# Filler products on TensorE in three waits of an audio-tower kernel (one core)

## The reference

```python
h = conv1d(x, W_embed, 7 taps, pad 3) + b_embed          # 64 x 32 x 4096
h = einsum('oc,bcl->bol', W_proj, fold16(h)) + b_proj     # 64 x 128 tokens x 256 channels
h = h + mamba(layernorm(h))      # W_in 256->1024, 4-tap conv, silu, selective scan over 128
                                 # tokens with 16 states, gate silu(z), W_out 512->256
n = layernorm(h)
gates = softmax(n @ w_gate); top 2 of 8 experts
h = h + sum over the chosen e of gate_e * (silu(n @ wg[e]) * (n @ wi[e])) @ wo[e]
```

## Time and profile before

| | us |
|---|---|
| median of 3 runs | 2648.08 (2647.75 to 2649.83) |
| the profiled execution | 2650.71 |
| its span, first to last instruction | 2648.9 |
| mean granted TensorE clock, as a share of full speed | 0.989 |

### The profile page before, as it was taken

The page is one execution under the profiler, slowest core; times in us unless marked ns, Lnnn a source line. Parts: engine busy times, 40 slices in busy tenths (PEclk is TensorE's granted clock), DMA queues, the critical chain, the costliest instruction groups (busy, mean ns, idle before and its releaser), DMA issues. The chain is left out here.

```text
span 2648.9 us, 35497 instructions
## 1 busy us (share of the span) xinstructions
PE 2469.8 (93%) x10678; PEld 1511.3 (57%) x10679; DVE 2025.5 (76%) x2052; ACT 1559.3 (59%) x3388; POOL 1929.2 (73%) x823
## 2 busy tenths in 40 slices
PE   4899999999999999999999999987599999999998
PEld 2334444444444444444444444433599999999998
DVE  1699999999999999999999999999333333333333
ACT  2677777777777777777777777764222222222222
POOL 2698999999999999999999999998322222222222
PEclk9999999999999999999999999999699999999999
DMA  2331414324143141431414314132532223222322
GB/s 44 141 116 43 157 39 154 116 59 158 38 154 117 58 158 38 154 120 55 158 38 154 122 53 156 39 141 88 189 47 48 46 46 48 46 47 46 47 47 33
DMA packets 124947, 235.85 MB, mean 89 GB/s; under 512 B 46031, under 2 KB 93170, under 8 KB 108460
## 3 DMA queue, kind: packets, MB, share of 16 engines
q1 hardware_dynamic: 96384, 199.06, 22.3%
q0 software_dynamic: 26272, 34.44, 7.7%
q10 hardware_dynamic: 2188, 1.15, 0.2%
HBM read 181.83 MB, written 53.65 MB: 89 GB/s over the span
## 5 line engine op out<-in xcount | busy, mean ns | idle before, releaser
L561 POOL TENSOR_TENSOR arena<-u,arena 128x2048 f32<-128x2048 f32 x255 | 1156.4, 4535 | 44.9 <-DVE psum L1180 41.2
L1180 DVE TENSOR_TENSOR_SCAN psum<-psum,arena 128x1024 f32<-128x1024 f32 x416 | 951.1, 2286 | 64.2 <-POOL arena L557 51.8
L1642 PE MATMUL psum<-hc,ident 128*128 128x512 f32 x1664 | 800.1, 605 | 95.0 <-DVE hc L1214 94.9
L891 ACT ACTIVATE psum<-delta,a_neg 128x508 f32<-128x508 f32 x1024 | 654.5, 670 | 0.0
L652 POOL DMA_INDIRECT out_dram<-hres,tok_id x135 | 210.6, 1560 | 548.1 <-ACT hres L1107 371.5
L1642 PEld LDWEIGHTS psum<-hc,ident 128*128 128x128 f32 x1664 | 298.1, 190 | 491.5 <-issue 290.7
L1214 DVE TENSOR_TENSOR hc<-psum,arena 128x1024 f32<-128x1024 f32 x416 | 507.8, 1221 | 9.9 <-PE psum L1642 0.9
L1481 DVE TENSOR_TENSOR z<-psum,xn 128x512 f32<-128x512 f32 x135 | 93.3, 691 | 432.6 <-issue 320.4
L1107 ACT ACTIVATE hres<-psum,tok_w 128x256 f32<-128x256 f32 x135 | 64.1, 475 | 400.4 <-PE psum L1817 382.6
L885 ACT ACTIVATE psum<-zeros 128x8 f32<-128x8 f32 x512 | 89.5, 175 | 303.4 <-DVE hc L1214 258.0
L1804 PE MATMUL psum<-xnt,yz 128*128 128x128 f32 x2160 | 264.9, 276 | 0.0
(11 more groups left out here) (219 smaller groups left out, 2840.5 us busy)
## 6 DMA issues: line engine op xcount, KB each, us to landing
arena<-ssm_rows SPq DMA_DIRECT2D x128, 1024.0 KB, 5.8
delta<-expert_rows SPq DMA_DIRECT2D x135, 129.0 KB, 2.0
h_saved_rows<-hnew SPq DMA_DIRECT2D x16, 512.0 KB, 6.8
hres<-h_saved_rows SPq DMA_DIRECT2D x16, 512.0 KB, 3.5
out_dram<-h SPq DMA_DIRECT2D x16, 512.0 KB, 2.9
arena<-in_L_ffn_wg_dram SPq DMA_DIRECT2D x8, 512.0 KB, 10.2
arena<-in_L_ffn_wi_dram SPq DMA_DIRECT2D x8, 512.0 KB, 10.8
arena<-in_L_ffn_wo_dram SPq DMA_DIRECT2D x8, 512.0 KB, 10.8
```

The costliest lines, as they stand in the source:

```text
L561: pool.tensor_tensor(dBx[k % 2], rep, b_rep[:, q * QN:(q + 1) * QN, :], ALU.mult).then_inc(dbx_ready, 1)
L891: last = nc.scalar.activation(o, d, ACT.Exp, scale=a_neg[:, c, n:n + 1])
L1180: nc.vector.tensor_tensor_scan(out_, h, src, 0.0, ALU.mult, ALU.add).then_inc(scan_done, 1)
L1642: last = nc.tensor.matmul(yacc[c % 2], ident[:, :], state[:, i, :], start=False, stop=(nth_sum[k] == LAST_SUM[c] and i == 1))
```

## The change

A helper issues `n` products of the identity with itself into bank 4 of `psum`, 128 columns. Nothing reads them and they signal nothing. It is called three times: 64 products ahead of TensorE's first work, behind a wait for all nine constants (it was one constant, and stood behind the wait for the transfers); 46 after the embedding of group 0 and ahead of `turn_xn(0, 0)`; and 42 behind the waits for `tab_ready` and `w_loaded`, ahead of `turn_tile(0, 0)`.

```diff
         def _(pe):
 
+            def keep_turning(n):
+
+                for _ in range(n):
+                    nc.tensor.matmul(psum[:, 4, 0:P], ident[:, :], ident[:, :], start=True, stop=True)
+
+            pe.wait_ge(s_const, 9)
+            keep_turning(64)
             pe.wait_ge(s_emb, 16 * N_EMB)
-            pe.wait_ge(s_const, 1)
             pe.wait_ge(s_band0, 3)
...
                 for m in range(2):
                     embed(0, m)
+                keep_turning(46)
                 pe.wait_ge(emb_free, 1)
                 for k in range(NK):
                     turn_xn(0, k)
...
             pe.wait_ge(tab_ready, 1)
             pe.wait_ge(w_loaded, 16 * 3 * E)
+            keep_turning(42)
```

## The result

| | before | after |
|---|---|---|
| median of 20 runs, us | 2649.57 (2646.9 to 2651.77) | 2652.91 (2651.0 to 2654.87) |
| ratio after / before | | 1.0013 (95%: 1.0007 to 1.0019) |
| span of the profiled execution, us | 2648.9 | 2652.8 |
| mean granted TensorE clock | 0.989 | 0.989 |

The change costs 0.13%, 3.3 us (95%: 1.9 to 5.0). The interval leaves out zero, but the cost is less than the 0.2% that the prediction took as no change. The spans of the two profiled executions differ by 3.9 us, and two places make all of it. Each trace is one execution: the one before took 2650.71 us, 1.1 above the median of its kernel, and the one after 2654.59, 1.7 above.

What follows compares the result with a forecast made beforehand. TensorE was taken as the bound from the first tile to the end, so delays show in full: front 1.9 plus first tile 0.3 makes 2.2 us later, 2650.3 from 2648.08; range 2645.5 to 2654, likeliest case 2648 to 2652.5.

Steps and rivals of the forecast that it cites:

- the overrun of the second call: Front: 46 fillers end at 45.4, turn_xn another 2.8 us late, but hidden because group 1's windows land only at 53.1.
- rival B: Front: clock falls again in TensorE's 2.9 us wait for group 1's landing; sum 4.9 us, 2653.0; chance 0.23.
- Price of a filler: All three calls: two records a product, 0.223 us at high clock, plus 0.477 us per low-clock microsecond, taken as 5.4.
- Rivals A: All three calls: clock does not rise on identity products or only on real work; about 37 us slower, 2685; chance 0.06.
- C: All three calls: a product leaves one record, so prices are half; sum -2.5 us, 2645.6; chance 0.09.
- The chain to SP's issues: Front: first call delays group 0's turning to end at 31.9 against 28.42, so SP's issues and landing are 3.4 us later.
- Behind the fillers the clock is high: Front after the first call: work runs at the high clock, with embeddings at 1.12 us each for 2.07 and 2.04.
- the overrun is hidden behind SP's transfers: Front: projection ends at 50.2, windows land at 53.1; without that cover the second call would cost 2.8 us.
- L1518 was to move with L349: Sign for group 1: L349 at about 31.9, L1518 at 53.1 behind a transfer; wrong if L1518 does not move with it.
- The stretch to the convolution: Front, from group 1's landing to the convolution: 2.65 us at the high clock instead of 4.12, a gain of 1.45.
- The first tile: Third call, ahead of tile 0: 3.2 us late, 2.9 gained by the high clock, net 0.3 us later.
- What lies between: From the front's end to tab_ready: unchanged time, no wait has slack to take up the front's delay.

Runs made afterwards that it cites:

- kernel with the waits filled: The changed kernel with 13 more products in five short waits between the first call and the second; 2653.12 us, ratio 1.0010.
- fitted kernel: Changed kernel with calls of 30, 32, 27 products, waits filled with 3, 13, 3, 3, 3, and 25 ahead of group 1's turning; 2645.83 us, ratio 0.9986.
- fitted kernel with separate memory: The fitted kernel with group 1's windows in memory of their own and 11 products instead of 25 ahead of their turning; 2647.18 us, ratio 0.9990.
- two queues: Fitted kernel with separate memory, half of group 1's issues on POOL, no products ahead of group 1's turning; 2649.85 us, ratio 1.0000.

## Why the prediction was right, and where it was not

- **Sign and size**: 2650.3 from a median of 2648.08 was +2.2 us; measured +3.3 (1.9 to 5.0), and 2652.91 is inside the range. Of the 2.6 us between 2650.3 and 2652.91, 1.5 lie in the median of the kernel before, which was 2648.08 over 3 runs and 2649.57 over 20. The sign came out right because the first and the third call last longer than the waits that they stand in, by prices that the traces bear out. What the prediction held to be hidden, the overrun of the second call, was not.
- **Luck in a number**: rival B gave 2653.0, almost the measured time, but by a fall of the clock in a wait for the landing that did not exist in the changed kernel. That match means nothing.
- **Price of a filler**: two records, 0.223 us at the high level and 0.477 us for each microsecond at the low one. First call 16.9 predicted, 17.2 and 17.0 measured; third 12.0, and 12.1 and 12.2 measured. Rivals A (37 us) and C (-2.5) are out by this. The first call's 128 records took 16.05 to 17.18 us over five traces, so 16.9 is good to about 1 us.
- **The chain to SP's issues**: 31.9 predicted, 32.03 and 31.89. That the landing follows at a fixed distance (21.3 us) held in the kernel with the waits filled: 31.33 to 52.76, 21.4.
- **The step that failed**: "Behind the fillers the clock is high", on which the embeddings at 1.12 each rest, and from it "the overrun is hidden behind SP's transfers". The clock fell at 32.4, 5.4 us after the call had ended, in a stretch in which TensorE worked in short groups between copies of ScalarE. The embeddings took 2.07 and 2.04, the second call 12.99 for 10.3, and the overrun came out 1.4 us beyond the landing. The front was 3.59 us late for 1.9 predicted, and this is most of the difference. One of the prediction's own signs of being wrong was met: L1518 was to move with L349, and moved 5.12 us (49.72 to 54.84) for 3.57. Filling the waits took the 1.4 us away in both traces, though not measurably in the time. Rival B had the fall, but at another place.
- **The stretch to the convolution**: 2.65 predicted, 2.59 measured.
- **The first tile**: 3.2 late, 2.9 back, 0.3 net predicted and read in the trace after; 0.4 net with the third call alone.
- **What lies between**: that no wait behind the front takes up its delay held: 1829.77 and 1829.75 us from the convolution to the last table instruction.
- The Trainium skill's rule that the full clock does not engage for transposes, "TensorE: Matmul & The Clock Gate", Part 4: the runs speak against it here. Four transposes take 0.60 us at 26.86 where they took 1.12 at 19.20.

## What to carry to other kernels

A filler must end before the work it precedes, at the low clock's price: compute its length as products at the high level plus the loss of the first 3 to 6 us at the low one (what the traces here show), and if in doubt take fewer. A filler call only helps if the clock is still up where the long products stand; where the work between is sparse, small fillers in the waits can hold it, as they did here in the traces. The fitted kernel has both, shorter runs and fillers in the waits, and which of the two gives how much of its 3.7 us was not measured apart. And look at what else waits behind the delayed engine: here TensorE began its first work 7.7 us late, and 3.6 us of that reached the end through a queue of transfers that nobody on TensorE computes with for another 20 us. Last, read one trace with care: places that an edit had not touched moved by up to 1.5 us.

## What the runs showed of the hardware

- The moment of the rise varies from trace to trace, least between two traces of one kernel (17.18 and 17.04, 16.49 and 16.38 us for 128 records). The same 60 records from 9.84 took 8.70, 9.87 and 9.76 us in three kernels, and 54 records ahead of the first tile 8.96, 9.13, 7.66 and 8.71. By the two prices, less 0.16 us of drain, that is an estimated 3 to 6 us at the low level, which alone moves a time by about 1.5 us.
- The column of the granted clock says 1.00 until the first recorded change, while durations there are those of the low level: in the kernel before it is 1.00 for 45 to 48 us, where the projection takes 3.75 us. Judge a start by durations.
- Waits of the same size ended differently: 2.76 us ahead of group 1's turning left the clock high. In the fitted kernel with separate memory it fell behind a wait of 3.11 us, at 50.1, when TensorE had been at work again for 0.9 us. With two queues it fell at 29.4, within the wait of 4.99 us.
- Each 21.8 KB transfer of windows took SP's queue about 2.4 us together with its one-row companion (sixteen issues from 28.46 to 48.26 in the kernel before). When two queues issued them together, single issues were held longer, up to 10.7 us on SP.
